# Loads in the order of use, with a signal per group, in an eight-stage cross-attention kernel

## The reference, cut to what matters

```python
def block_forward(x, context, g1, be1, wq1, wk1, wv1, wo1, bo1, ...):    # L0, and L1 alike
    x = cross_attention(layer_norm(x, g1, be1), layer_norm(x, g1, be1), wq1, wk1, wv1, wo1, bo1) + x
    x = cross_attention(layer_norm(x, g2, be2), context, wq2, wk2, wv2, wo2, bo2) + x
    return geglu_ff(layer_norm(x, g3, be3), w_ff1, b_ff1, w_ff2, b_ff2) + x

def geglu_ff(x, w1, b1, w2, b2):
    h = jnp.einsum('bne,ef->bnf', x, w1) + b1
    a, gate = (h[..., :DFF], h[..., DFF:])        # DFF = 1280
    h = a * jax.nn.gelu(gate)
    return jnp.einsum('bnf,fe->bne', h, w2) + b2
```

## Time and profile before

| | us |
|---|---|
| median of 3 runs | 4276.19 |
| lowest and highest run | 4259.37, 4277.89 |
| the profiled execution | 4277.93 |
| its span in the trace | 4276.0 |
| TensorE busy in the span | 3827.7 (90%) |
| VectorE, ScalarE, GpSimd busy | 1717.3, 1544.2, 665.1 |
| mean granted TensorE clock | 0.932 of full speed |

### The profile page before, as it was taken

The page is one execution under the profiler, slowest core; times in us unless marked ns, Lnnn a source line. Parts: engine busy times, 40 slices in busy tenths (PEclk is TensorE's granted clock), DMA queues, the critical chain, the costliest instruction groups (busy, mean ns, idle before and its releaser), DMA issues.

```text
span 4276.0 us, 40948 instructions
## 1 busy us (share of the span) xinstructions
PE 3827.7 (90%) x16744; PEld 1579.3 (37%) x16744; DVE 1717.3 (40%) x2274; ACT 1544.2 (36%) x2149; POOL 665.1 (16%) x419
## 2 busy tenths in 40 slices
PE   7999899997989899997997999999879978878997
PEld 2333333333333333333443333333324445443333
DVE  1534335242534435351123555665512122235553
ACT  2424343342524343440112555555511111115553
POOL 1413223141413223240000000000000000000000
PEclk9999999999989999998998999999989976658999
DMA  2000000001000000001001000000010010000000
GB/s 79 15 15 23 11 23 4 26 12 45 16 13 22 10 22 4 29 7 48 0 1 37 1 1 5 5 5 1 1 48 1 0 31 8 4 23 5 5 1 25
DMA packets 39961, 67.46 MB, mean 16 GB/s; under 512 B 5088, under 2 KB 27552, under 8 KB 39264
## 3 DMA queue, kind: packets, MB, share of 16 engines
q1 hardware_dynamic: 39776, 64.85, 5.2%
HBM read 62.22 MB, written 2.62 MB: 15 GB/s over the span
## 4 chain that ended last, share of the span: by engine, by line
PE 78%; DVE 12%; ACT 3%; DMA 3%; issue 3%; SPq 1%; POOL 0%; ACTq 0%; DVEq 0%
PE bank L469 11%; PE bank L402 7%; PE bank L547 7%; DVE heads L849 6%; PE bank L436 5%; PE bank L888 5%; PE bank L522 5%; PE bank L835 4%; PE bank L1351 4%; PE bank L1353 3%; PE bank L1002 3%; DVE negm L499 2%; PE bank L815 2%; PE bank L491 2%; PE bank L940 2%
## 5 line engine op out<-in xcount | busy, mean ns | idle before, releaser
L849 DVE TENSOR_REDUCE heads<-bank 128x2 f32<-128x1024 f32 x480 | 588.2, 1225 | 527.6 <-PE bank L835 526.3
L499 DVE TENSOR_REDUCE negm<-bank 128x2 f32<-128x1024 f32 x320 | 387.9, 1212 | 960.3 <-PE bank L491 960.3
L402 PE MATMUL bank<-weights,mixed 128*128 128x320 f32 (+1 forms) x1376 | 405.2, 454 | 19.6 <-DVE mixed L1378 12.4
L522 PE MATMUL bank<-weights 64*128 64x512 f32 x1280 | 409.6, 625 | 0.0
L469 PE MATMUL bank<-hT,heads 128*128 128x512 f32 x720 | 382.1, 652 | 16.8 <-issue 9.6
L402 PEld LDWEIGHTS bank<-weights,mixed 128*128 128x128 f32 (+1 forms) x1376 | 264.5, 197 | 163.8 <-issue 25.9
L581 DVE RECIPROCAL rec<-ox 128x128 f32<-128x128 f32 x320 | 279.0, 918 | 90.0 <-ACT ox L586 84.3
L815 PE MATMUL bank<-heads 32*128 32x512 f32 x1920 | 305.2, 633 | 6.2 <-ACT probs L862 2.3
L835 PE MATMUL bank<-heads 32*128 32x512 bf16 x960 | 190.7, 394 | 87.7 <-DVE heads L849 83.1
L558 POOL TENSOR_TENSOR heads<-probs 128x1024 f32<-128x1024 f32 x40 | 96.5, 2413 | 843.9 <-ACT probs L537 843.9
L1378 DVE SCALAR_TENSOR_TENSOR mixed<-bank,b_col,probs 128x512 f32<-128x512 f32 x80 | 60.1, 751 | 391.5 <-ACT probs L1367 391.5
(11 more groups left out here) (177 smaller groups left out, 5433.7 us busy)
## 6 DMA issues: line engine op xcount, KB each, us to landing
heads<-in_wqk SPq DMA_DIRECT2D x40, 384.0 KB, 3.0
heads<-in_wqk SPq DMA_DIRECT2D x40, 320.0 KB, 2.9
ctx_in<-in_ctx SPq DMA_DIRECT2D x16, 384.0 KB, 3.4
weights<-in_L_xattn_wo SPq DMA_DIRECT2D x2, 1600.0 KB, 9.4
x_res<-in_x SPq DMA_DIRECT2D x1, 2560.0 KB, 9.9
weights<-in_L_xattn_w_ff SPq DMA_DIRECT2D x1, 2560.0 KB, 15.3
weights<-in_L_xattn_ff_w SPq DMA_DIRECT2D x1, 2560.0 KB, 15.6
out<-x_res SPq DMA_DIRECT2D x1, 2560.0 KB, 8.7
```

The costliest lines, as they stand in the source:

```text
L402: last = nc.tensor.matmul(M.SM[t % 2][:, 0:D], v["OT"][0:w, c, t * P:t * P + P], v["wo"][0:w, c, :], start=c == 0, stop=c == nch - 1)
L499: nc.vector.tensor_reduce(M.negm[:, u % 2, i, 0:2], M.ROWS[:, :, :], AX.X, ALU.max, negate=True).then_inc(s.sem("max"), 1)
L522: nc.tensor.matmul(out[:, g, :], v["KT"][strip, u % 3, i * P:i * P + P], v["QT"][strip, u % 3, :], start=True, stop=False)
L849: nc.vector.tensor_reduce(v["negm"][:, qb, 64 * half:64 * half + 64].rearrange("p (g k) -> p g k", g=2)[:, :, 0], M.ROWS4[:, :, :], AX.X, ...
```

## The change

Nothing of the computation changes. The loads are split, put in another order, and signalled by groups.

- x is loaded in four pieces. The first batch raises a semaphore of its own, `x_first`, which only VectorE's first norm waits for. The other three are issued behind `wv` of stage 0 and raise `x_done` by 48 in all, the new `X_IN`. VectorE waits for that before it makes the norm of the second batch.
- In stage 0 the first two `wqk` tiles are issued ahead of all other weights. The function `pair_weights` has the two statements that stood in the loop of `attention_sync`.
- `g` and `be` raise a semaphore `gb` (in all stages with a norm but 3 and 4), and ScalarE waits for this one before the first chunk of hT. `wv` of a "big" attention stage raises `wv_in`, which `values_pe` waits for. TensorE waits for `w_in` only ahead of the output projection in such a stage.
- `wv` is issued ahead of `wo` in all attention stages.
- In the feed-forward stages `b1` comes right behind `bo`. `w1` follows in three blocks of 2, 3 and 5 tiles of units, each by four loads with a semaphore for each block, which `ff_pe` waits for at the block's first tile of the first batch. w2 comes last with its own semaphore, waited for ahead of the first batch's output projection.

```diff
--- before.py
+++ after.py
@@ -29,7 +29,7 @@
 EPS = 1e-5
 CH = [(0, 128), (128, 128), (256, 64)]
 CCH = [(0, 128), (128, 64)]
-X_IN = 16
+X_IN = 48
 NTOK = 16
 
 
@@ -115,6 +115,7 @@
     with ExitStack() as ctx:
         M = Memory(nc, ctx)
         stats, mv, vare, rstd, xn, xcopy = (ctx.enter_context(nc.semaphore(n)) for n in ("stats", "mv", "vare", "rstd", "xn", "xcopy"))
+        x_first = ctx.enter_context(nc.semaphore("x_first"))
         x_done = ctx.enter_context(nc.semaphore("x_done"))
         consts = ctx.enter_context(nc.semaphore("consts"))
         masks = ctx.enter_context(nc.semaphore("masks"))
@@ -146,6 +147,8 @@
 
         def start(eng, s, b):
 
+            if s.index == 0 and b == 0:
+                return
             hold(eng, x_done, after(b, TB, (s.index * B - s.first) * TB + X_IN))
 
 
@@ -227,21 +230,43 @@
                     a, w = chunks[full]
                     load(dst[0:w, full, :], src[a:a + w, :])
 
+            def load_values():
+                full = 2 * P if not p["cross"] else P
+                sp.dma_start(v["wv"][:, 0:full // P, :], p["wv"][0:full, :].rearrange("(c p) f -> p c f", p=P)).then_inc(s.sem("wv_in" + s.tag), 16)
+                sp.dma_start(v["wv"][0:64, full // P, :], p["wv"][full:full + 64, :]).then_inc(s.sem("wv_in" + s.tag), 16)
+
             if p["ln"]:
-                load(v.get("g", M.g_col[:, :]), p["g"])
-                load(v.get("be", M.b_col[:, :]), p["be"])
+                if s.index in (3, 4):
+                    load(v["g"], p["g"])
+                    load(v["be"], p["be"])
+                else:
+                    sp.dma_start(M.g_col[:, :], p["g"]).then_inc(s.sem("gb" + s.tag), 16)
+                    sp.dma_start(M.b_col[:, :], p["be"]).then_inc(s.sem("gb" + s.tag), 16)
             load(v.get("bo", M.bo_row[:, :]), p["bo"].rearrange("(a d) -> a d", a=1).broadcast_to([P, D]))
+            if s.kind == "ff":
+                load(M.b1_col[:, :], p["b1"])
+                s.n_loads = n
+                for k, (j0, j1) in enumerate(FF_BLOCKS):
+                    for half in range(2):
+                        f = slice(half * DFF + j0 * P, half * DFF + j1 * P)
+                        sp.dma_start(v["w1"][:, 0:2, f], p["w1"][0:2 * P, f].rearrange("(c p) f -> p c f", p=P)).then_inc(s.sem(f"w1_{k}"), 16)
+                        rows = slice(0, 64) if half else slice(64, P)
+                        sp.dma_start(v["w1"][rows, 2, f], p["w1"][2 * P:D, f]).then_inc(s.sem(f"w1_{k}"), 16)
+                sp.dma_start(v["wo"], p["wo"].rearrange("(c p) f -> p c f", p=P)).then_inc(s.sem("wo_in"), 16)
+                return
+            if s.kind == "att" and p["big"]:
+                load_values()
+            elif s.kind == "att":
+                load_chunks(v["wv"],  p["wv"], kv_chunks(s))
+            if s.index == 0:
+                for b in range(1, B):
+                    sp.dma_start(M.x[:, b * TB:b * TB + TB, :], io["x"][b * N:b * N + N, :].rearrange("(t p) d -> p t d", p=P)).then_inc(x_done, 16)
             load_chunks(v["wo"], p["wo"], out_chunks(s))
             if s.kind == "att":
-                load_chunks(v["wv"], p["wv"], kv_chunks(s))
+                pass
                 if not p["big"]:
                     load_chunks(v["wq"], p["wq"], CH)
                     load_chunks(v["wk"], p["wk"], kv_chunks(s))
-            elif s.kind == "ff":
-                load(v["w1"][:, 0:2, :], p["w1"][0:2 * P, :].rearrange("(c p) f -> p c f", p=P))
-                load(v["w1"][0:64, 2, DFF:2 * DFF], p["w1"][2 * P:D, DFF:2 * DFF])
-                load(v["w1"][64:P, 2, 0:DFF], p["w1"][2 * P:D, 0:DFF])
-                load(M.b1_col[:, :], p["b1"])
             else:
                 load_chunks(G["wq"], p["wq"], CH)
                 for k in ("wk", "wkd", "wv", "wvd"):
@@ -281,6 +306,7 @@
             o2 += n
 
 
+        FF_BLOCKS = [(0, 2), (2, 5), (5, 10)]
         LN_BATCHES = sum(s.prm["ln"] for s in stages) * B
 
         def overall(s, b):
@@ -314,6 +340,8 @@
         def norm_next_dve(dve, s, b):
 
 
+            if s.index == 0 and b == 0:
+                dve.wait_ge(x_done, X_IN)
             if s.prm["ln"]:
                 norm_dve(dve, overall(s, b) + 1, (b + 1 - s.first) % B)
 
@@ -363,7 +391,7 @@
                 act.wait_ge(s.sem("in_ps" + s.tag), after(b - s.first, n_in(s), k + 1))
                 if s.prm["ln"]:
                     if c == 0:
-                        act.wait_ge(s.w_in, 16 * s.n_loads)
+                        act.wait_ge(s.sem("gb" + s.tag), 32)
                     ins = nc.scalar.activation(M.hT[0:w, c, :], M.PJ[k % 2][0:w, :], ACT.Identity,
                                                bias=M.b_col[0:w, c:c + 1], scale=M.g_col[0:w, c:c + 1])
                 else:
@@ -391,7 +419,9 @@
                     for t in range(TB):
                         last = nc.tensor.transpose(M.PJ[c % 2][0:w, t * P:t * P + P], v["On"][:, t, a:a + w], M.ident[:, :])
                     last.then_inc(s.sem("ot_ps"), 1)
-            if not s.prm.get("big"):
+            if s.prm.get("big"):
+                pe.wait_ge(s.w_in, 16 * s.n_loads)
+            else:
                 pe.wait_ge(s.sem("ot"), after(b, nch, nch))
             for t in range(TB):
                 if t >= 2:
@@ -426,7 +456,7 @@
 
             v, dh, sl, kv = V[s.name], s.prm["dh"], v_slices(s), kv_chunks(s)
             if t == 0:
-                pe.wait_ge(s.w_in, 16 * s.n_loads)
+                pe.wait_ge(s.sem("wv_in" + s.tag), 32)
                 hold(pe, s.sem("in_evac" + s.tag), after(b - s.first, n_in(s), n_in(s)))
             for j, (h0, nh) in enumerate(sl):
                 k = t * len(sl) + j
@@ -1321,19 +1351,29 @@
             sp.dma_start(M.ctx_in[:, :, :], io["ctx"][bass.ts(b - s.first, N), :].rearrange("(t p) d -> p t d", p=P)
                          ).then_inc(s.sem("ctx_in" + s.tag), 16)
 
+        def pair_weights(sp, s, b, u):
+            sp.wait_ge(s.sem("k_ps"), after(b, PAIRS, u - 1))
+            sp.dma_start(V[s.name]["wqk"][:, u % 2, :, :],
+                         s.prm["wqk"][u * P:u * P + P, :].rearrange("p (c f) -> p c f", f=P)).then_inc(s.sem(f"wqk{u % 2}"), 16)
+
         def attention_sync(sp, s):
+            if s.index == 0:
+                pair_weights(sp, s, 0, 0)
+                pair_weights(sp, s, 0, 1)
             load_weights(sp, s)
             for b in range(s.first, s.first + B):
                 start(sp, s, b)
                 if s.prm["cross"]:
                     load_context(sp, s, b)
-                for u in range(PAIRS):
-                    sp.wait_ge(s.sem("k_ps"), after(b, PAIRS, u - 1))
-                    sp.dma_start(V[s.name]["wqk"][:, u % 2, :, :],
-                                 s.prm["wqk"][u * P:u * P + P, :].rearrange("p (c f) -> p c f", f=P)).then_inc(s.sem(f"wqk{u % 2}"), 16)
+                for u in range(2 if s.index == 0 and b == 0 else 0, PAIRS):
+                    pair_weights(sp, s, b, u)
 
 
         NF = DFF // P
+
+        def ff_weights(pe, s, what):
+
+            pe.wait_ge(s.sem(what), (64 if what != "wo_in" else 16) * (1 + s.first // B))
 
         def ff_pe(pe, s):
             v = V[s.name]
@@ -1343,6 +1383,10 @@
                 pe.wait_ge(s.w_in, 16 * s.n_loads)
                 hold(pe, s.sem("in_evac" + s.tag), after(b - s.first, 3, 3))
                 for j in range(NF):
+                    if b == s.first:
+                        for k, (j0, _) in enumerate(FF_BLOCKS):
+                            if j == j0:
+                                ff_weights(pe, s, f"w1_{k}")
                     if j >= 2:
                         pe.wait_ge(s.sem("ot"), after(b, NF, j - 1))
                     gate, lin = M.ST[j % 2], M.PJ[j % 2]
@@ -1353,6 +1397,8 @@
                         nc.tensor.matmul(lin[:, :], v["w1"][:, e, af], M.hT[:, e, :], start=e == 0, stop=False)
                     nc.tensor.matmul(gate[:, :], v["w1"][0:64, 2, gf], M.hT[0:64, 2, :], start=False, stop=True).then_inc(s.sem("g_ps"), 1)
                     nc.tensor.matmul(lin[:, :], v["w1"][64:P, 2, af], M.hT[64:P, 2, :], start=False, stop=True).then_inc(s.sem("a_ps"), 1)
+                if b == s.first:
+                    ff_weights(pe, s, "wo_in")
                 out_pe(pe, s, b)
 
         def ff_act(act, s):
@@ -1548,7 +1594,7 @@
 
         @block.sync
         def _(sp):
-            sp.dma_start(M.x[:, :, :], io["x"].rearrange("(t p) d -> p t d", p=P)).then_inc(x_done, X_IN)
+            sp.dma_start(M.x[:, 0:TB, :], io["x"][0:N, :].rearrange("(t p) d -> p t d", p=P)).then_inc(x_first, 16)
             for s in stages:
                 if s.index in runs:
                     narrow_sync(sp, runs[s.index])
@@ -1623,7 +1669,7 @@
             nc.vector.tensor_copy(M.mask[64:P, 2:3], M.mask[64:P, 1:2]).then_inc(masks, 1)
             for s in stages:
                 if s.index == 0:
-                    start(dve, s, 0)
+                    dve.wait_ge(x_first, 16)
```

## The result

| | before | changed |
|---|---|---|
| median, us | 4275.15 (4 runs) | 4221.52 (4 runs, 4201.86 to 4252.28) |
| profiled execution, us | 4277.93 | 4201.86 |
| its span, us | 4276.0 | 4200.0 |
| its mean granted clock | 0.932 | 0.939 |

The ratio is 0.9889, with a 95% interval of 0.985 to 0.9929: the changed kernel is 1.1% faster. The forecast was 4226 us. The two traces differ by 76 us and the medians by 54, because the trace of before is of one of its longer runs and the trace of the changed kernel is of its shortest. So the traces are used for places and for the length of single batches, and the medians for the whole.

A forecast was written before the change was run, and what follows sets the result against it. TensorE, 78% of the last chain, was taken as the bound, so loads matter only where it waits. Gains 16.3 + 0.9 + 16.4 + 16.5 = 50.1 us off 4277.9, less 1.7 for the median, gave 4226 us; range 4206 to 4249.

The forecast's parts named there:

- rows 2 to 6: Profile rows for four places: ScalarE waits there for every load of the stage, though it needs two columns of 1.5 KB.
- start: Start of stage 0: first projection at 16.5 instead of 32.77 us, gain 16.3 us, bounds 14.0 and 16.8.
- stage 1: Only hT is freed, so TensorE transposes the context when it lands: gain 0.9 us, bounds 0 and 1.5.
- stage 2: Feed-forward: matmuls start at 1947.2 instead of 1963.66 us, gain 16.4 us, bounds 13.7 and 17.9.
- stage 5: Feed-forward, same loads as stage 2: gain 16.5 us, bounds 13.8 and 17.9.
- What was said to be hidden: Later loads (rest of x, wv, wo, blocks 1 and 2, w2) land before they are wanted: no cost.
- Rival 1: Feed-forward stages: block 0's small loads are served one by one, gain 9.4 us each, total 4240 us; chance 0.13.
- Rival 2: Start: x's first batch shares the queue equally with what follows, 5.5 us less gain, 4232 us; chance 0.08.
- Rival 3: Stage 6: the clock drops to 1.2 GHz throughout, 109 us more, 4335 us; chance 0.05 for slower or near no change.
- Rival 4: Feed-forward stages: first tiles run at the full clock, 2 x 2.0 us more gain, 4222 us; chance 0.2.
- all of it counts: Whole kernel: the holes lie on TensorE's chain, which bounds it right behind each, so the full 50.1 us is gained.

The follow-up runs named there:

- e3: Changed kernel with w1 in three large loads and one signal instead of twelve loads in three blocks, order kept: 4249.29 us, ratio 0.9968.
- e6: Changed kernel with x in one load, still first in the queue: 4221.86 us, ratio 0.9925.
- e7: Changed kernel with 22 extra matmuls of no use to the result at the start of each feed-forward stage: 4235.14 us, ratio 0.9949.
- e11: Changed kernel with context and pairs ahead, w1 stored by tiles, and first loads of stages 1, 2, 5 issued in the stage before: 4128.7 us, ratio 0.9672.
- e2: Kernel before with only the feed-forward stages 2 and 5 changed: 4234.22 us, ratio 0.9938.
- e1: Kernel before with only the start of stage 0 changed: 4246.97 us, ratio 0.9960.
- e12: Changed kernel with five extra matmuls in the pause for loads at each later batch of stages 0 and 1: 4197.98 us, ratio 0.9837.
- e4: Changed kernel with the context and first two wqk of stage 1 ahead of wv and wo: 4206.27 us, ratio 0.9874.

## Why the prediction was right, and where it was off

**The waits that the change takes apart.** Four holes on TensorE, each ended by a load that was not needed: that reading of rows 2 to 6 held. In each place the time until dense work begins fell by what was forecast or a little more.

| term of the sum | forecast, us | in the trace, us |
|---|---|---|
| start, 32.77 to 16.51 | 16.3 | 16.3 |
| stage 1, projection after `g` issued: 21.06 to 19.02 | 0.9 | 2.0; 1.5 by the first `values_pe` |
| stage 2, 24.23 to 7.14 | 16.4 | 17.1, less 0.9 for the first tile |
| stage 5, 24.35 to 7.36 | 16.5 | 17.0, less 0.1 for the first tile |
| sum | 50.1 | some 51, and 53.0 by the four batches |

The steps between them held too: the norm at 5.04 (forecast 5.2), transposes at 11.20 (11.4), ScalarE at 12.45 (12.4), the projection at 16.51 (16.5), block 0 there 7.1 us after `g` (7.8). The 0.7 us at block 0 are the issues: they took 0.43 to 0.59 us each, where the rows of before had left up to 0.99 open. In stage 1, the context landed after 13.4 us, and TensorE takes it at once instead of 0.9 us later. The gain there is larger than forecast because the context is also issued 2.9 us after `g` instead of 3.7.

**What was said to be hidden was hidden.** No wait for the rest of x, `wv`, `wo`, the blocks 1 and 2, or w2 stands in the trace.

**Rival 1, small loads one by one,** is refuted by the landings of 3.6 to 3.7 us for four loads issued within 2 us, and e3 shows that the split earned what the forecast gave it. **Rival 2, x's first batch not served first,** is refuted by the norm at 5.04; e6 gives its price, 5.5 us, just the figure of the prediction. The later pieces paid instead: SP was held 4.64 us in the issue of three of them, and `wo` went out at 9.45. **Rival 3, the clock of stage 6,** did not come: 0.67 and 0.66 in the two traces, after 0.65. **Rival 4, first tiles at the full clock,** did not come: the clock fell in two pauses of some 3 us as it had in one of 20. e7 shows that the mechanism is real and worth 2 to 3 us a stage, but its filler delayed the first tile by more. e11, with no pause, had it for nothing.

**What was off.** The sum of the holes is 51 to 53 us, and the medians of the first comparison say 54. But over the three series of experiments the kernel before has a mean of 4263.4 (66 runs, 4234 to 4292), and the changed kernel's 13 runs have one of 4224.2 (4202 to 4252): 39 us, with an error of some 9, and 35 in the one series that has nine of the 13. So about 12 us of the traced gain were given back, and that the first result met the forecast of 4226 so closely was partly luck: the forecast started from three runs with a median of 4276, which is 13 us above the mean of the many. The step that did not hold in full is the sentence that all of it counts, since the kernel is bound by TensorE right behind each hole. It is, but not at a constant clock. Within one kernel, 0.001 of mean granted clock goes with 3.5 us, which covers nearly all that its runs scatter (what is left has a deviation of 2.7 us). The holes of stages 2 and 5 had lain at a low clock: 33 us at 0.64 from 1939 and from 3127 before, 16 us at 0.68 from 1906 and from 3078 now. Taking them away should raise the mean clock by 2 x (33 x 0.36 - 16 x 0.32) / 4224 = 0.003. It is 0.9348 in the runs of before and 0.9347 in those of the changed kernel, and 0.003 is 11 us.

Most of this can be found in the first batches of stages 0 and 1, over all traces that have the same loads and waits there (stage 0: before, its repeat and e2, against all others but e6; stage 1: before, its repeat, e1 and e2, against changed, its repeat, e7, e3, e6 and e12):

| first batch of | loads as before | loads as changed |
|---|---|---|
| stage 0 | 268.2 to 270.1 (3 traces, mean 268.9) | 253.1 to 259.2 (10 traces, mean 256.2) |
| stage 1 | 240.1 to 242.0 (4 traces, mean 240.6) | 238.9, 239.0, 239.2, 250.4, 250.5, 250.7 (mean 244.8) |

By these means the start gains 12.7 us instead of 16.3, and stage 1 loses 4 instead of gaining 1 to 2: together 9 of the 12 us. The mean of 244.8 comes from six values in two groups and may be off by 5. In stage 1 TensorE waits some 12 us for the context in all six traces of the last column. The clock is at 0.50 when dense work begins and comes back 7 us after the wait in the changed kernel, but 36 us after it in e6. The window from 10 to 33 us behind the end of that wait shows it, in the changed kernel and then in e6:

```profile
1003.00:1027.00 24.00, 24.00 (x59) 7.67 (x57) 4.62 (x4) 7.85 (x15) 0.00 (x0) 1.00 0.06 16
1010.00:1034.00 24.00, 24.00 (x30) 7.13 (x30) 0.28 (x1) 4.16 (x8) 0.00 (x0) 0.50 0.05 14
```

This is the same as at the turns. The two traces of the changed kernel itself both have the short form, e3, e6 and e12 the long one. The four traces with stage 1 as before all have 20 us at 0.50, and none has the long form. Whether the change makes the long form more frequent, or three of six is chance, stays open.

## What to carry to other kernels

Ask of each wait for a load what the waiting instruction reads, and put that first in the queue, inputs as well as weights, with a signal of its own: here four such places were worth some 39 us, one more load put forward 9 more in its batch, and loads issued before the stage ends took the rest of the holes away. Count a pause of TensorE not only by its length: at the turns of the batches under 3 us of waiting cost up to 17 at the low clock, and what kept TensorE from pausing there gained some 60 us (loads issued a batch ahead, in stage 6 too) and some 25 (five idle matmuls). A gain of 1% wants more runs than four where the clock makes the runs scatter by 1%.

## What the runs showed of the hardware that was not expected

- After a pause of 2.6 or 2.7 us at a turn the granted clock fell to 0.50 and came back after some 7 us in one batch (the changed kernel at 1219) and after some 34 us in another (the kernel before at 1241), with TensorE busy with the same instructions. After a wait of 12 us it came back 7 us into dense work in one trace and 36 us into it in another (the changed kernel and e6, stage 1). So equal batches take 225 to 227 or 237 to 242 us.
- A 256 KB load in a row of small ones landed 3.7 us after its issue, 384 KB alone took 3.0: several at a time cost hardly more than one. The context's 384 KB took 6.4 us behind 160 KB (e4) and 13.4 behind 2.8 MB.
- The issues of stage 2 on SP took 0.33 to 0.67 us each, but at the start three issues for x took 4.64 us together and the next one 2.04, with 3.2 MB issued ahead of the first and 5.2 MB ahead of the last. That the amount still in the queue held them up is likely, and not shown.
- The queue does not run evenly at the start. This row of the changed kernel, 0 to 60 in slices of 1.5 us, has 400 GB/s and more for the first pieces and 160 to 260 in stretches between; the forecast had read a steady 380 from the same row of before, and nothing came late for it.

```profile
GB/s 0 81 400 415 162 264 433 322 163 212 352 363 364 363 361 288 26 0 0 0 0 0 168 94 0 0 0 0 0 0 0 0 11 0 0 0 25 238 0 0
```
